# Scaling of streamed units moved from ScalarE to GpSimd, and the halo's edge copied from the halo buffer one tile later

## The chip, the cores and the metric

The kernel runs on one core of a Trainium2 chip. The metric is the device time of one execution in microseconds (us), which the slowest core sets; here there is one core. Lower is better.

## The reference

The input x is (1, 16, 2048, 2048) in float32. Two layers follow each other:

```
x = x + conv(groupnorm(x), weight)     # 8 groups of 2 channels; depthwise 6 x 11, causal: the
                                       # lower triangle of input and output alone is kept
x = x + groupnorm(x) + bias            # bias[c, i, j] = table[i - j], from a small MLP, per channel
```

The second line is `out = x * s + (bias + t)` with two numbers s and t for each group of channels. They are known only once the whole group has gone through the convolution. The part of x above the diagonal is not changed by the first line, but it too takes the second.

## The kernel before

A group is two channels. A channel is cut into four bands of 512 rows: the partition is a row block of four rows, so a band is 128 partitions x 4 rows x columns. A band's lower part is walked in **tiles** of 118 new columns: 5, 9, 13 and 18 tiles for the four bands, 90 tiles a group, 720 in all. For each tile ScalarE normalizes (`norm`, line 553), GpSimd masks it where it lies on the diagonal (`mask_tile`, line 951, 42 of 90 tiles), TensorE transposes it (line 1033), ScalarE casts the result to a high half in f16 (`split_hi`, line 568), VectorE makes the low half (`split_lo`, line 707), TensorE runs 36 matmuls (line 1047), and VectorE masks and adds the result into x (`evict`, lines 720 and 722). XT, the transposed tile, has three buffers, as have psT and psY.

The convolution needs two columns of XT from the band above. They are kept in `halo`, one entry for each tile position t. GpSimd copies them into XT in front (`halo_from`, line 966) and takes the last two out afterwards (`halo_to`, line 974). Where a band's width is no whole number of tiles, the next band needs two columns of a tile position that this band does not have. They are moved between partitions by four small DMAs (`copy_edge`, lines 572 to 579), from the XT buffer of the band's last tile. This occurs for one tile of each channel (tiles 26 and 71 of a group), 16 times in all. XT's buffer is written again three tiles on, so `split_hi` of that tile waits for `edge_copied`.

All five engines run one program that is unrolled over the 90 tiles of a group and loops over groups. Each pass does three things at once: statistics of group g+1 (part A, VectorE line 735, loads into `abuf`), the convolution of group g (part B), and the second layer of group g-1 (part C). Part C has kept blocks that stay in memory (`finish_kept`, line 874) and 36 **streamed units** of 512 KB for each group. A unit is loaded by SyncE into one of four buffers `ubuf` (line 469), finished there, and stored by ScalarE's queue (`store_stream`, line 619). 13 of the 36 are finished on VectorE in one instruction (`finish_stream`, line 882). The other 23 take two: ScalarE multiplies by s (`scale_stream`, line 612), then GpSimd adds the bias (`add_bias`, line 982). Over 8 groups that is 184 units.

A planner (`plan`) gives each unit the tile at which it is loaded, finished and stored: the load is issued two tiles ahead, the store stands two tiles behind, and the next load into a buffer waits for that buffer's store. Each engine executes its own list in order. Within tile n ScalarE has: `split_hi(n+2)`, `norm(n+4)`, the edge's copy, two squares for the statistics (line 590), the scaling of a unit, stores. GpSimd has: `mask_tile(n+4)`, `halo_to(n+1)`, `halo_from(n+2)`, `add_bias` of a unit. So an engine that waits for a unit's load holds up its share of the tiles behind it.

Of the kernel before, what the change touches and what calls it, by code (L numbers as in the profile page):

```python
# [25 lines left out]
def preact_conv_kernel(nc, x, wflip, w1, b1, w2, b2, w3, b3, out):  # L26
# [12 lines left out]
    XC = P // K  # L39
# [203 lines left out]
    with ctx:  # L243
# [277 lines left out]
        def _(act):  # L521
# [38 lines left out]
            def split_hi(g, n):  # L560
                N = NT * g + n
                act.wait_ge(transposed, N + 1)
                wait(act, convolved, N - NB3 + 1)
                wait(act, halo_out, N - NB3 + 1)
                for e, _ in EDGES:
                    if n == e + NB3:
                        act.wait_ge(edge_copied, 16 * K * (NEDGE * g + edges_before(n)))
                nc.scalar.copy(XT[:, n % NB3, 0, :, 2:P + 2], psT[n % NB3][:, :, :]).then_inc(hi_ready, 1)  # L568

            def copy_edge(g, n, w):  # L570

                c, b, t = TILES[n]
                act.wait_ge(lo_ready, NT * g + n + 1)
                act.wait_ge(halo_zeroed, chan(g, c) + 1)
                piece_i, col = divmod(STEP, XC)
                for k in range(K):
                    act.dma_start(halo[XC * k:XC * k + w, t + 1, :, 0, :],
                                  XT[XC * k + col:XC * k + col + w, n % NB3, :, piece_i, P:P + 2]
                                  ).then_inc(edge_copied, 16)
# [27 lines left out]

            def scale_stream(g, u):

                v = ubuf[:, u % NUB, :, :]  # L610
                act.wait_ge(u_loaded[u % NUB], 16 * (g * (NU // NUB) + u // NUB + 1))
                nc.scalar.activation(v, v, ACT.Identity, scale=col(outp, 0)  # L612
                                     ).then_inc(u_scaled, 1)
# [8 lines left out]
            def stage(s, do_a, do_b, do_c, do_next):  # L622
                p, ga, gb, gc = plan(do_a, do_b, do_c, on_dve), s, s - 1, s - 2
                for n in range(NT):
# [16 lines left out]
                    if do_b:  # L641
                        for e, w in EDGES:
                            if e == n:
# [10 lines left out]
                    if do_c:  # L654
# [9 lines left out]
                        for u in range(NU):  # L664
                            if p.u[u] == n and not on_dve[u]:
                                scale_stream(gc, u)
# [263 lines left out]
        def _(pool):  # L930
# [37 lines left out]
            def halo_to(g, n):  # L968
# [4 lines left out]
                wait_alone(pool, lo_ready, N + 1)  # L973
                nc.gpsimd.tensor_copy(halo[:, t, :, :, :], XT[:, n % NB3, :, :, P:P + 2]).then_inc(halo_out, 1)  # L974

            def add_bias(g, u):
                c = STREAM[u][0]
                if u_before[0][u] == u_before[0][c * (NU // CPG)]:
                    wait_alone(pool, bias_shifted, chan(g, c) + 1)
                pool.wait_ge(u_scaled, N_POOL * g + u_before[0][u] + 1)  # L980
# [149 lines left out]
```

## Time and profile before

| | us |
|---|---|
| median of 3 runs | 2881.85 (2877.08 to 2887.26) |
| the profiled execution, its own time | 2876.63 |
| its span, first to last instruction | 2874.8 |
| TensorE / VectorE / ScalarE / GpSimd busy | 2028.4 / 2305.3 / 1675.5 / 1159.4 |
| granted TensorE clock, mean share of 2.4 GHz | 0.893 |
| moved by DMA | 916.67 MB, mean 319 GB/s |

Part B runs from about 144 to 2710 us. The passes of the loop repeat with a period of about 337 us. The last 165 us are part C of the last group alone. Rows name a group of instructions by line, engine and operation, with what it writes and reads (`out<-in`). "Idle before" is time in which the engine had nothing running just before them, with what ended it. ACT is ScalarE, DVE is VectorE, POOL is GpSimd, PE is TensorE and SP is SyncE; a name with q is the engine's sequencer, which also issues DMAs.

### The profile page before, as it was taken

How to read it: one execution, taken by the hardware profiler on the slowest of the kernel's cores; microseconds unless marked ns; L12 is line 12 of the kernel's file. 1: busy time of each engine (PE TensorE's matmuls, PEld its weight loads, DVE VectorE, ACT ScalarE, POOL GpSimd, SP SyncE). 2: the span in 40 equal slices, each digit the busy share in tenths (PEclk: the TensorE clock that was granted, in tenths of full speed). 3: DMA queues.
4: the chain of work that ended last, by engine and by line, in shares of the span. 5: the costliest groups of instructions: out<-in, count | busy, mean ns of one | idle time of the engine just before them, and what ended most of it. 6: DMA issues, size and time to landing. Idle time of an engine off the chain costs nothing.

```text
span 2874.8 us, 82154 instructions
## 1 busy us (share of the span) xinstructions
PE 2028.4 (71%) x28880; PEld 1920.2 (67%) x28880; DVE 2305.3 (80%) x4167; ACT 1675.5 (58%) x3051; POOL 1159.4 (40%) x1988
## 2 busy tenths in 40 slices
PE   4089887778677775878668776787768777888600
PEld 0089886777577775867668776677758677778500
DVE  6878888798787987889787997879888897858625
ACT  2067665666557564766556665566647656677621
POOL 1033224534435343353435433453533535555443
PEclk9999998999889998999889999899989999999855
DMA  8875848999799987999889997999979996788799
GB/s 255 305 250 191 297 159 315 382 345 341 261 395 350 366 318 274 394 343 361 293 302 383 339 351 279 360 375 346 343 278 410 327 382 239 277 292 308 274 350 346
DMA packets 319859, 916.67 MB, mean 319 GB/s; under 512 B 42864, under 2 KB 42864, under 8 KB 317520
## 3 DMA queue, kind: packets, MB, share of 16 engines
q1 hardware_dynamic: 203744, 595.03, 58.3%
q10 hardware_dynamic: 115840, 318.80, 28.9%
q14 instruction: 204, 1.67, 0.2%
q8 instruction: 71, 1.16, 0.2%
HBM read 594.18 MB, written 319.68 MB: 318 GB/s over the span
## 4 chain that ended last, share of the span: by engine, by line
DMA 32%; DVE 25%; issue 17%; PE 10%; ACT 9%; POOL 3%; ACTq 2%; SPq 1%; DVEq 0%; POOLq 0%
DMA ubuf<-in_x 8%; DVE entries L735 8%; PE psY L1047 8%; DMA out<-ubuf 7%; DVE kept_c_band L874 5%; DMA abuf<-in_x 4%; DMA out<-kept_c_band 4%; DMA kept_c_band<-in_x 4%; DVE XT L707 4%; DVE psY L720 3%; DMA halo<-XT 3%; ACT junk L590 2%; ACT XT L568 2%; PE psT L1033 2%; ACT xn L553 2%
## 5 line engine op out<-in xcount | busy, mean ns | idle before, releaser
L1047 PEld LDWEIGHTS psY<-wsplit,XT 128*128 128x128 f16 x25920 | 1635.3, 103 | 299.3 <-issue 98.7
L1047 PE MATMUL psY<-wsplit,XT 128*128 128x168 f16 (+5 forms) x25920 | 1661.4, 225 | 234.3 <-DVE band L722 98.3
L707 DVE TENSOR_TENSOR XT<-psT,XT 128x512 f16<-128x512 f32 x720 | 491.0, 682 | 357.0 <-ACT XT L568 355.4
L1033 PE MATMUL psT<-ident,xn 128*128 128x128 f32 x2880 | 496.3, 298 | 326.9 <-POOL xn L951 224.2
L568 ACT CAST XT<-psT 128x512 f16<-128x512 f32 x720 | 414.9, 576 | 530.7 <-PE psT L1033 252.8
L982 POOL TENSOR_TENSOR ubuf<-ubuf,bias 128x1024 f32<-128x1024 f32 x184 | 412.2, 2241 | 523.7 <-ACT ubuf L612 523.4
L735 DVE BATCH_NORM_STATS2 entries<-abuf 128x6 f32<-128x512 f32 x928 | 586.8, 680 | 43.0 <-DMA abuf<-in_x 42.5
L951 POOL TENSOR_TENSOR xn<-xn,mask 128x512 f32<-128x512 f32 x336 | 416.3, 1239 | 503.9 <-ACT xn L553 422.3
L1033 PEld LDWEIGHTS psT<-ident,xn 128*128 128x128 f32 x2880 | 328.1, 150 | 342.3 <-POOL xn L951 221.9
L974 POOL COPY halo<-XT 128x16 f16<-128x16 f16 x720 | 222.5, 309 | 643.3 <-DVE XT L707 630.9
L553 ACT ACTIVATE xn<-kept_c_band,normp 128x512 f32<-128x512 f32 (+2 forms) x496 | 398.6, 804 | 94.8 <-DMA kept_c_band<-in_x 78.3
L874 DVE SCALAR_TENSOR_TENSOR kept_c_band<-kept_c_band,outp,bias 128x1024 f32<-128x1024 f32 x224 | 345.5, 1555 | 38.6 <-ACT bias L662 38.6
L612 ACT ACTIVATE ubuf<-ubuf,outp 128x1024 f32<-128x1024 f32 x184 | 209.7, 1140 | 253.2 <-DMA ubuf<-in_x 169.5
L590 ACT ACTIVATE junk<-kept_c_band,cur 128x512 f32<-128x512 f32 (+2 forms) x464 | 311.9, 672 | 66.0 <-DVE kept_c_band L722 31.1
L722 DVE SCALAR_TENSOR_TENSOR kept_c_band<-psY,wback,kept_c_band 128x472 f32<-128x472 f32 (+3 forms) x496 | 343.8, 693 | 6.2
L882 DVE SCALAR_TENSOR_TENSOR ubuf<-ubuf,outp,bias 128x1024 f32<-128x1024 f32 x104 | 159.3, 1532 | 98.2 <-DMA ubuf<-in_x 65.8
L720 DVE TENSOR_TENSOR psY<-psY,mask 128x472 f32<-128x472 f32 (+2 forms) x336 | 203.7, 606 | 0.0
L553 ACT ACTIVATE xn<-band,normp 128x512 f32<-128x512 f32 (+1 forms) x224 | 174.3, 779 | 28.4 <-DVE normp L801 28.4
L966 POOL COPY XT<-halo 128x16 f16<-128x16 f16 x720 | 166.2, 231 | 31.1 <-PE psY L1047 27.3
L590 ACT ACTIVATE junk<-band,cur 128x512 f32<-128x512 f32 x192 | 132.0, 687 | 40.4 <-DVE cur L806 21.8
L722 DVE SCALAR_TENSOR_TENSOR band<-psY,wback,band 128x472 f32<-128x472 f32 (+2 forms) x224 | 150.4, 671 | 5.6
L590 ACT ACTIVATION_READ_ACCUMULATOR junk<-kept_c_band,cur 128x1 f32 x464 | 87.0, 188 | 0.0
(76 smaller groups left out, 440.7 us busy)
## 6 DMA issues: line engine op xcount, KB each, us to landing
abuf<-in_x SPq DMA_DIRECT2D x464, 512.0 KB, 7.0
out<-ubuf ACTq DMA_DIRECT2D x288, 512.0 KB, 6.1
kept_c_band<-in_x SPq DMA_DIRECT2D x224, 512.0 KB, 8.7
out<-kept_c_band ACTq DMA_DIRECT2D x224, 512.0 KB, 7.2
ubuf<-in_x SPq DMA_DIRECT2D x192, 512.0 KB, 6.3
band<-in_x SPq DMA_DIRECT2D x48, 1024.0 KB, 9.5
out<-band ACTq DMA_DIRECT2D x48, 1024.0 KB, 9.3
ubuf<-out SPq DMA_DIRECT2D x96, 512.0 KB, 7.0
```

What stands on the lines that cost most here:

```text
L553: last = nc.scalar.activation(to[:, :, 0:whole, :], slot(c, b)[:, :, x0:x0 + XC * whole].rearrange("p k (i c) -> p k i c", c=XC), ACT.Iden ...
L568: nc.scalar.copy(XT[:, n % NB3, 0, :, 2:P + 2], psT[n % NB3][:, :, :]).then_inc(hi_ready, 1)
L590: nc.scalar.activation(junk[:, 0:nr * (c1 - c0)].rearrange("p (r c) -> p r c", r=nr), slot(c, b)[:, r:r + nr, BW * q + c0:BW * q + c1], AC ...
L707: nc.vector.tensor_tensor(XT[:, n % NB3, 1, :, 2:P + 2], psT[n % NB3][:, :, :], XT[:, n % NB3, 0, :, 2:P + 2], ALU.subtract).then_inc(lo_r ...
L720: nc.vector.tensor_tensor(y, y, mask_at(b, t, c0, c1), ALU.mult).then_inc(conv_masked, 1)
L722: nc.vector.scalar_tensor_tensor(out=xs, in0=y, scalar=col(wback, c), in1=xs, op0=ALU.mult, op1=ALU.add, accum_out=sums[:, n:n + 1]).then_ ...
L735: last = nc.vector.bn_stats(entries[:, e, :], row(q, r))
L874: nc.vector.scalar_tensor_tensor(out=v, in0=v, scalar=col(outp, 0), in1=bias_at(blk, nr // 2 * h, nr // 2), op0=ALU.mult, op1=ALU.add).the ...
L951: nc.gpsimd.tensor_tensor(v, v, m, ALU.mult).then_inc(xn_ready, 1)
L982: nc.gpsimd.tensor_tensor(v, v, bias_at(STREAM[u]), ALU.add).then_inc(u_added, 1)
L1033: last = nc.tensor.transpose(psT[m][:, i, :], xn[:, m, i, :, :].rearrange("p k c -> p (k c)"), ident[:, :])
L1047: last = nc.tensor.matmul(psY[m][:, 0:rows, o + lo_c:o + hi_c], XT[:, m, xp, i, 2 - sh:2 - sh + P], wsplit[:, c, wp, K * sh:K * sh + rows, ...
```

## The change

Two parts. First, `scale_stream` goes from ScalarE's list; `add_bias` on GpSimd now waits for the unit's load, multiplies by s in place, waits for that instruction, and adds the bias. Second, `copy_edge` reads the two columns from the `halo` entry that `halo_to` has written, not from XT, and stands one tile later in ScalarE's list. It waits for `halo_out` in place of `lo_ready` and `halo_zeroed`. `split_hi` no longer waits for `edge_copied`. The `halo` entry that the DMA reads is overwritten by the next band, so `halo_to` waits for `edge_copied` there, twice a group.

```diff
@@ split_hi (ScalarE)
                 wait(act, halo_out, N - NB3 + 1)
-                for e, _ in EDGES:
-                    if n == e + NB3:
-                        act.wait_ge(edge_copied, 16 * K * (NEDGE * g + edges_before(n)))
                 nc.scalar.copy(XT[:, n % NB3, 0, :, 2:P + 2], psT[n % NB3][:, :, :]).then_inc(hi_ready, 1)
@@ copy_edge (ScalarE)
-                act.wait_ge(lo_ready, NT * g + n + 1)
-                act.wait_ge(halo_zeroed, chan(g, c) + 1)
+                act.wait_ge(halo_out, NT * g + n + 1)
                 piece_i, col = divmod(STEP, XC)
                 for k in range(K):
                     act.dma_start(halo[XC * k:XC * k + w, t + 1, :, 0, :],
-                                  XT[XC * k + col:XC * k + col + w, n % NB3, :, piece_i, P:P + 2]
-                                  ).then_inc(edge_copied, 16)
+                                  halo[XC * k + col:XC * k + col + w, t, :, piece_i, :]).then_inc(edge_copied, 16)
@@ stage (ScalarE)
                         for e, w in EDGES:
-                            if e == n:
+                            if e + 1 == n:
                                 copy_edge(gb, e, w)
...
-                        for u in range(NU):
-                            if p.u[u] == n and not on_dve[u]:
-                                scale_stream(gc, u)
@@ halo_to (GpSimd)
+                for e, _ in EDGES:
+                    if n > e and (c, t) == (TILES[e][0], TILES[e][2]):
+                        wait_alone(pool, edge_copied, 16 * K * (NEDGE * g + edges_before(n)))
                 nc.gpsimd.tensor_copy(halo[:, t, :, :, :], XT[:, n % NB3, :, :, P:P + 2]).then_inc(halo_out, 1)
@@ add_bias (GpSimd)
+                wait_alone(pool, u_loaded[u % NUB], 16 * (g * (NU // NUB) + u // NUB + 1))
+                flat_v = ubuf[:, u % NUB, :, :]
+                nc.gpsimd.tensor_scalar(flat_v, flat_v, col(outp, 0), None, ALU.mult).then_inc(u_scaled, 1)
                 pool.wait_ge(u_scaled, N_POOL * g + u_before[0][u] + 1)
                 v = unit_of(ubuf, u % NUB, STREAM[u])
                 nc.gpsimd.tensor_tensor(v, v, bias_at(STREAM[u]), ALU.add).then_inc(u_added, 1)
```

ScalarE's list in the loop, at the first edge of a group (tile 26), before. The third row is the issue of the edge's first DMA, and line 568 is the cast into XT:

```order
L568 CAST XT<-psT 128x4x128 [waits halo_out,convolved,transposed]
L553 ACTIVATE xn<-kept_c_band,normp 128x4x4x32 [waits transposed]
L577 DMA halo<-XT 2x2x2 [waits halo_zeroed,lo_ready]
L577 DMA halo<-XT 2x2x2 x3
L562 REGISTER_ALU
L567 REGISTER_ALU [waits halo_out,convolved,transposed]
L568 CAST XT<-psT 128x4x128 [waits edge_copied]
L553 ACTIVATE xn<-kept_c_band,normp 128x4x4x32 [waits transposed]
```

And of the changed kernel, where the cast is line 565 and the edge's DMA line 573:

```order
L565 CAST XT<-psT 128x4x128 [waits halo_out,convolved,transposed]
L553 ACTIVATE xn<-kept_c_band,normp 128x4x4x32 [waits transposed]
L565 CAST XT<-psT 128x4x128 [waits halo_out,convolved,transposed]
L553 ACTIVATE xn<-kept_c_band,normp 128x4x4x32 [waits transposed]
L573 DMA halo<-halo 2x2x2 [waits halo_out]
L573 DMA halo<-halo 2x2x2 x3
```

The cast that stood behind the four DMAs and waited for their landing now stands in front of them, and no cast waits for `edge_copied`.

GpSimd's list in the loop at a unit on diagonal tiles, before (974 and 966 are the two halo copies, 951 the mask, 982 the bias addition):

```order
L974 COPY halo<-XT 128x16 [waits halo_in,lo_ready]
L966 COPY XT<-halo 128x8x2 [waits convolved]
L980 REGISTER_ALU
L982 TENSOR_TENSOR ubuf<-ubuf,bias 128x1024 [waits u_scaled]
L947 REGISTER_ALU
L951 TENSOR_TENSOR xn<-xn,mask 128x512 [waits diag_normed]
```

And of the changed kernel (962 and 951 are the halo copies, 936 the mask, 970 the new scaling, 973 the addition):

```order
L962 COPY halo<-XT 128x16 [waits halo_in,lo_ready]
L951 COPY XT<-halo 128x8x2 [waits convolved]
L379 ISA
L970 TENSOR_SCALAR ubuf<-ubuf,outp 128x1024 [waits u_loaded0]
L971 REGISTER_ALU
L973 TENSOR_TENSOR ubuf<-ubuf,bias 128x1024 [waits u_scaled]
L932 REGISTER_ALU
L936 TENSOR_TENSOR xn<-xn,mask 128x512 [waits diag_normed]
```

GpSimd now waits for the load itself, and the mask and halo copies of the next tile stand behind two instructions of the unit where they stood behind one.

## Rows read from the trace of the kernel before

**Rows 1.** The page's busy times and shares of the span.

```profile
PE 2028.4 (71%) x28880; PEld 1920.2 (67%) x28880; DVE 2305.3 (80%) x4167; ACT 1675.5 (58%) x3051; POOL 1159.4 (40%) x1988
```

**Rows 2.** The page's chain that ended last, shares of the span.

```profile
DMA 32%; DVE 25%; issue 17%; PE 10%; ACT 9%; POOL 3%; ACTq 2%; SPq 1%; DVEq 0%; POOLq 0%
DMA ubuf<-in_x 8%; DVE entries L735 8%; PE psY L1047 8%; DMA out<-ubuf 7%; DVE kept_c_band L874 5%; DMA abuf<-in_x 4%; DMA out<-kept_c_band 4%; DMA kept_c_band<-in_x 4%; DVE XT L707 4%; DVE psY L720 3%; DMA halo<-XT 3%; ACT junk L590 2%; AC
```

**Rows 3.** Stage windows: width, PE PEld DVE ACT POOL busy, clock, DMA share, GB/s.

```profile
1140.00:1260.00 120.00, 98.70 (x1416) 95.33 (x1415) 96.73 (x179) 81.14 (x150) 55.46 (x97) 0.90 1.00 381
...
1340.00:1412.00 72.00, 51.63 (x730) 49.33 (x731) 62.77 (x115) 45.59 (x83) 35.77 (x56) 0.91 0.88 321
...
2710.00:2875.00 165.00, 0.59 (x2) 0.50 (x2) 74.16 (x63) 36.20 (x37) 54.78 (x23) 0.51 0.93 342
```

**Rows 4.** The waits: waiter <- releaser: us in total, times, longest.

```profile
POOL ubuf L982 <- ACT ubuf L612: 523.4, 136, 16.5
...
DVE XT L707 <- ACT XT L568: 355.4, 247, 6.2
...
PE psT L1033 <- POOL xn L951: 224.2, 88, 10.6
...
ACT ubuf L612 <- DMA ubuf<-in_x: 169.5, 53, 7.9
...
ACT XT L568 <- DMA halo<-XT: 80.8, 16, 6.2
...
ACT ubuf L612 <- DMA ubuf<-out: 39.7, 12, 5.5
```

**Rows 5.** Timeline at the first edge of a group: start, us, what, [idle before].

```profile
1197.92 1.28 DVE L882 SCALAR_TENSOR_TENSOR ubuf<-ubuf,outp,bias 128x1024 f32<-128x1024 f32 x1
...
1198.60 2.12 PE L1047 MATMUL psY<-wsplit,XT 128*128 128x148 f16 x36
...
1200.84 0.58 ACT L568 CAST XT<-psT 128x512 f16<-128x512 f32 x1 [5.67 <-DMA halo<-XT]
...
1203.59 0.58 PE L1047 MATMUL psY<-wsplit,XT 128*128 128x148 f16 x7 [0.74 <-DVE kept_c_band L722]
```

**Rows 6.** Timeline at a unit whose load lands late.

```profile
1240.85 1.15 ACT L612 ACTIVATE ubuf<-ubuf,outp 128x1024 f32<-128x1024 f32 x1 [5.08 <-DMA ubuf<-in_x]
1241.06 0.34 ACTq L619 DMA_DIRECT2D out<-ubuf  x1
...
1242.08 2.35 POOL L982 TENSOR_TENSOR ubuf<-ubuf,bias 128x1024 f32<-128x1024 f32 x1 [4.83 <-ACT ubuf L612]
...
1244.39 1.13 POOL L951 TENSOR_TENSOR xn<-xn,mask 128x512 f32<-128x512 f32 x1
...
1245.57 1.12 PE L1033 MATMUL psT<-ident,xn 128*128 128x128 f32 x4 [5.27 <-POOL xn L951]
```

**Rows 7.** The page's groups: count, busy us, mean ns, idle before.

```profile
L982 POOL TENSOR_TENSOR ubuf<-ubuf,bias 128x1024 f32<-128x1024 f32 x184 | 412.2, 2241 | 523.7 <-ACT ubuf L612 523.4
...
L874 DVE SCALAR_TENSOR_TENSOR kept_c_band<-kept_c_band,outp,bias 128x1024 f32<-128x1024 f32 x224 | 345.5, 1555 | 38.6 <-ACT bias L662 38.6
L612 ACT ACTIVATE ubuf<-ubuf,outp 128x1024 f32<-128x1024 f32 x184 | 209.7, 1140 | 253.2 <-DMA ubuf<-in_x 169.5
...
L882 DVE SCALAR_TENSOR_TENSOR ubuf<-ubuf,outp,bias 128x1024 f32<-128x1024 f32 x104 | 159.3, 1532 | 98.2 <-DMA ubuf<-in_x 65.8
```

**Rows 8.** GpSimd's instructions with one input, by line: busy us, mean ns.

```profile
L939 POOL TENSOR_SCALAR_AFFINE_SELECT mask<-mask 128x728 bf16<-128x728 bf16 x1 | 0.8, 792 | 0.1
...
L941 POOL TENSOR_SCALAR_AFFINE_SELECT ident<-ident 128x128 f32<-128x128 f32 x1 | 0.3, 293 | 0.0
```

**Rows 9.** Timeline: GpSimd and VectorE instructions that meet.

```profile
1025.08 1.80 DVE L882 SCALAR_TENSOR_TENSOR ubuf<-ubuf,outp,bias 128x1024 f32<-128x1024 f32 x1
...
1025.74 1.20 POOL L974 COPY halo<-XT 128x16 f16<-128x16 f16 x1
...
1027.26 0.20 POOL L974 COPY halo<-XT 128x16 f16<-128x16 f16 x1 [0.19 <-POOL XT L966]
```

More of the change, by code:

```diff
@@ L606, in store_kept @@
                               ).then_inc(kept_stored[(blk, h)], 16)
[L608 to L613, printed above, removed]
             def store_stream(g, u):
```

## The prediction, made before the changed kernel had run

> **What bounds the kernel now.** I read the busy times first: no engine is full, VectorE is nearest with 80% of the span, ScalarE has 58% and GpSimd 40% [rows 1]. The chain of work that ended last says the same: DMA has 32% of it, VectorE 25%, ScalarE 9% and GpSimd 3% [rows 2]. Of the DMA part, the loads and stores of the streamed units have 8% and 7%, and the edge's small DMAs 3%. So the kernel is bound by turns. The stage windows tell where [rows 3]: from 1140 to 1260 us the 16 DMA engines are busy throughout (share 1.00, 381 GB/s), from 1340 to 1412 they have 12% to spare, and in the last 165 us, which hold part C alone, 7%. What is won in the first of these windows is mostly given back to the transfers; in the others it may stay.
>
> Then I read the waits [rows 4]. Two of ScalarE's belong to this change. It waits 16 times for the edge's DMAs, 80.8 us in all, and before the scalings for their loads, 169.5 us in 53 waits and 39.7 us in 12 more. VectorE waits 355.4 us for ScalarE's cast, which is one of the things queued behind both. TensorE waits 224.2 us in 88 waits for GpSimd's mask, and that is the part that a longer GpSimd list can make worse.
>
> **The edge.** The four DMAs are still issued, and cost ScalarE's queue the same; only the wait goes. The place shows what the wait does [rows 5]: a convolution ends at 1200.72 (1198.60 + 2.12), the cast could not start before 1200.84 after 5.67 us of idle time, and the next convolution starts at 1203.59, so TensorE lost 2.9 us. Sixteen times 2.9 us are 46 us. The limits are 0, if every wait is taken up by a later one, and the 76 us that 3% of the chain nearly comes to (I take 0.026 x 2875) [rows 2]; the full 80.8 us is the same thing read from the waits. Half of the 16 lie in the window with full DMA engines, and I give these a quarter of 23 us and the other eight a little over half of it: **-20 us**. The new waits cost nothing: `halo_out` of that tile was already awaited by the cast of three tiles on, which now stands in front, and `edge_copied` on GpSimd is awaited many tiles after the DMAs. If that cover went, each would cost one landing of some 5 us, on 16 tiles.
>
> **ScalarE loses the scaling.** It loses 184 instructions of 1.140 us, 209.7 us, and the idle time before them, 253.2 us [rows 7]. The loads that it waited for are not gone, they are now awaited by GpSimd, which waited for them before too, behind ScalarE. The example shows all of it [rows 6]. The load lands at 1240.85, the scaling takes 1.15, the addition runs from 1242.08 for 2.35 us, the mask follows at 1244.39, and only then can TensorE transpose, at 1245.57 after 5.27 us. Here TensorE is held by the load and GpSimd, not by ScalarE; putting 1.14 us on GpSimd in place of ScalarE changes nothing in it. But note the store of another unit, issued at 1241.06, 0.2 us after the load had landed: it stood behind ScalarE's wait. A late load of one buffer thus delays the store that frees another, whose load is late in turn. That coupling goes, because ScalarE next waits for this unit two tiles later, at its store. In the chain, loads and stores of units are 15% of 2875, some 430 us, and ScalarE 9% [rows 2]. With 65 such waits of 3.2 us (209.2 / 65), I take a sixth of their sum for the coupling in the loop, -35 us, and -5 us for the last stretch with its 7% to spare: **-40 us** together. The limits are 0 and all 209 us.
>
> **GpSimd gains an instruction for each unit.** The trace has no such instruction on GpSimd. Two with one input give a line: 293 ns for 128 elements and 792 ns for 728 [rows 8], so 0.83 ns an element, 1.04 us for 1024. They are of another operation and partly of another type, so this is an estimate. From below 0.85 us (the slope alone), from above 2.24 us, the addition over the same elements with two inputs [rows 7]. I take 1.1 us, near the one-input rows, and 0.2 us for the wait between it and the addition, as before a copy that waits for another one on this engine (0.19) [rows 9]. Three kinds of units:
> - 65 late loads: the unit is done 1.3 us after landing plus the addition, before 1.14 + 0.08. Half of that reaches TensorE: 65 x 0.08 x 0.5, **+3 us**.
> - 48 units (184 - 136 waits [rows 4]) where GpSimd was the late one: each is 1.3 us later, and with it the next tile's mask and halo. A quarter reaches TensorE, since most tiles wait for something else: 48 x 1.3 x 0.25, **+16 us**.
> - 71 units where ScalarE was late for another reason than the load: GpSimd did nothing and can now go ahead. It is early, which nobody waits for: 0, at most 1.3 us each the other way.
>
> **The two engines meet.** VectorE's instructions with two inputs from memory take 1.28 us alone [rows 5], but 1.80 us where they meet a GpSimd instruction, and a GpSimd copy of 0.20 us takes 1.20 behind one [rows 9]. Over 224 and 104 of them the means are 1.555 and 1.532 us, so 62 + 26 = 88 us are lost on VectorE beside GpSimd's 1159.4 us of work [rows 1, 7], 0.076 for each of them. 184 x 1.1 = 202 us more give 15 us, and with half of it on the path **+8 us**; the limits are 0 and, with 2.24 us in place of 1.1 and all of it on the path, 31.
>
> The Trainium skill, SBUF — State Buffer, section "SBUF: two separate sides", states that VectorE and GpSimd share one pair of ports by an exclusive lock, held for a whole instruction, between a VectorE operation with two SBUF inputs and any GpSimd operation that reads SBUF. By that rule the trace agrees (1.80 for 1.28, 1.20 for 0.20), and it says that the one-input scaling locks as the addition does; the sum above already counts it fully. The Trainium skill, GPSIMD Engine Reference, section "Engine selection", calls GpSimd's one-input operations roughly line-rate; at its clock of 1.2 GHz that would be an estimate of 0.85 us, and the sum would come out 13 us lower. No row here shows it.
>
> **The sum.** -20 - 40 + 3 + 16 + 8 = -33 us. Against the profiled execution's own 2876.6 us that is 2843.6. It lies 5 us under the median of the runs, 2881.85, so against the median it is 2849, and I give **2850 us**.
>
> **Rivals.** (A) *GpSimd's list becomes the wait.* The three costs together are 65 x 0.5 x (m - 1.02) + 48 x 0.25 x (m + 0.2) + 184 x 0.038 x m, or 51.5 m - 30.8 us with the new instruction's duration m. At 1.1 that is 26, at 2.24 it is 85 against the 60 won: 2882 + 25 = **2907 us**. It decides from m = 1.76 us, which either the instruction itself or its meetings with VectorE can reach. For it: 224 us of TensorE's waits already end at GpSimd's mask. Against it: GpSimd is at 40%, and the one-input rows lie at half of that price. Chance 0.22. (B) *The transfers take it all.* In the window with DMA share 1.00 neither gain nor cost shows; if the rest of the loop behaves alike, or if gains and costs cancel, the time is **2882 us** within 8. For it: 32% of the chain is DMA and 916.67 MB have to be moved either way. Chance 0.14. (C) *ScalarE was the coupling of everything.* Edge 76 us, coupling 60 us in place of 40, costs 26: 2882 - 110 = **2772 us**, or 2790 where part of the edge's is given back. For it: VectorE's 355.4 us behind the cast. Against it: the load-late example, where TensorE waits for GpSimd in both kernels. Chance 0.12. (D) *The wait moves to the store and back.* If GpSimd finishes a late unit more than two tiles after its landing, ScalarE stands at `u_added` with its casts behind it. Tiles take 337 / 90 = 3.75 us, two are 7.5, and load to sum takes 3.6, so this needs a GpSimd already 4 us behind; it is part of A's price.
>
> **Chances and range.** My case has 0.52, with 2828 to 2870 for its own range. A measurement of this kernel tells 0.3%, some 9 us, from no change. Faster by more than that: my case but for a small part, and C: 0.63. Within it: nearly all of B and the fringes of A and of mine: 0.14. Slower: A but for its fringe, and a bit of B: 0.23. The range goes from 2800 us, which takes in half the way to C and the bound 0.85 us, to 2900 us, which takes in B, and A up to m = 2.1 (51.5 x 2.1 - 30.8 - 60 = 17).
>
> **What would show it.** Right: no wait of the cast for the edge's DMA; the new instruction at 1.0 to 1.3 us; ScalarE's busy time down by 210 to about 1466 us; GpSimd's up by some 200 to 1360; GpSimd's wait before the scaling for loads, about 170 to 210 us in 50 to 65 waits; the means of VectorE's lines 874 and 882 up from 1.55 to 1.60 to 1.65; stores no longer issued right at a landing; TensorE's wait for the mask between 200 and 260 us. Wrong: a duration over 1.76 us, TensorE's wait for the mask over 300 us, or ScalarE idle at a unit's store for more than 50 us in all. If the cast waits less and the time stays, B was right and the loads' waits on GpSimd and VectorE will have grown.

## The result and the profile after

The changed kernel takes 2954.88 us (median of 4 runs, 2949.85 to 2961.34), the kernel before 2884.56 (4 runs). The ratio is 1.0248, 95% interval [1.0216, 1.028]: 2.5% slower, 71 us at the 2877 us to which I refer all ratios below. Forecast were 2850 us and a range up to 2900. The profiled execution has a span of 2959.6 us.

The page's busy times and its chain, engines first and then the first lines:

```profile
PE 2048.0 (69%) x28880; PEld 1950.5 (66%) x28880; DVE 2356.0 (80%) x4167; ACT 1490.3 (50%) x2867; POOL 1687.0 (57%) x2172
...
DVE 27%; DMA 21%; issue 17%; POOL 15%; PE 13%; ACT 5%; SPq 1%; ACTq 1%; POOLq 0%; DVEq 0%
...
PE psY L1038 10%; POOL ubuf L970 9%; DVE entries L720 9%; DVE kept_c_band L859 5%; DMA ubuf<-in_x 5%; DMA abuf<-in_x 4%; DMA out<-kept_c_band 4%; DVE XT L692 4%; PE psT L1024 3%; DVE psY L705 3%; DMA out<-ubuf 3%; DMA out<-band 3%; POOL ubuf L973 2%; POOL xn L936 2%; ACT junk L585 1%
```

Against [rows 1] ScalarE is busy 185 us less. That is short of the 210 us that its scalings take by their own durations, since in the trace of before they overlap their neighbours by 21 us. GpSimd is busy 528 us more, where some 200 were expected. Against [rows 2] DMA falls from 32 to 21% of the chain and GpSimd rises from 3 to 15%, of which the new scaling alone has 9.

GpSimd's groups, shapes kept apart (busy us, mean ns, then the idle time before them and what ended it):

```profile
L970 POOL TENSOR_SCALAR ubuf<-ubuf,outp 128x1024 f32<-128x1024 f32 x184 | 552.0, 3000 | 198.9 <-ACT bias L650 91.4 <-DMA ubuf<-in_x 89.3 <-DMA ubuf<-out 18.0
L973 POOL TENSOR_TENSOR ubuf<-ubuf,bias 128x1024 f32<-128x1024 f32 x184 | 421.6, 2292 | 15.4
L936 POOL TENSOR_TENSOR xn<-xn,mask 128x512 f32<-128x512 f32 x336 | 414.1, 1232 | 462.9 <-ACT xn L553 386.9 <-ACT xn L556 75.0
```

The new instruction takes **3.00 us, not 1.1**. It is longer than the addition with two inputs over the same unit (2.29 here, 2.24 before), which I had taken as its upper bound. The rest of GpSimd's difference is small.

The waits (waiter, releaser, us in total, times, longest) show who pays:

```profile
ACT XT L565 <- PE psT L1024: 552.0, 324, 6.1
...
DVE XT L692 <- ACT XT L565: 367.8, 249, 6.5
...
PE psT L1024 <- POOL xn L936: 321.2, 85, 10.8
...
ACT XT L565 <- POOL halo L962: 107.4, 55, 7.5
...
POOL ubuf L970 <- DMA ubuf<-in_x: 89.3, 25, 7.4
...
PE psY L1038 <- POOL XT L951: 72.3, 43, 4.7
```

The cast's wait for the edge's DMA (80.8 us in [rows 4]) is gone, as meant. But TensorE's wait for the mask has grown from 224.2 to 321.2 us, and the freed ScalarE spends its time waiting for TensorE's transposes. GpSimd itself waits less for loads than forecast (89.3 us in 25 waits, plus 18.0 for loads from the output), because it comes to most of them late.

Two windows, with the columns of [rows 3]:

```profile
1160.00:1280.00 120.00, 97.21 (x1411) 93.53 (x1408) 97.21 (x177) 69.08 (x137) 84.81 (x109) 0.91 0.96 365
2782.00:2960.00 178.00, 0.83 (x8) 0.64 (x5) 81.77 (x64) 10.37 (x15) 130.86 (x46) 0.51 0.87 317
```

The first lies at the same place of the program as 1140:1260 before, some 20 us on. The transfers, which had filled it (share 1.00, 381 GB/s), now leave 4% idle, and GpSimd's busy time has gone from 55 to 85 us of 120. The second begins where the last convolution ends, at 2782.2 where it was 2709.2. So 73 us of the span's 85 are lost in the loop. Of the other 12, the last part is 178 us long in place of 166, with GpSimd busy for 131 us where it was 55: there it is the one that the last stores wait for.

What happens in the loop, from the timeline of the changed kernel (start, us, what, and in brackets the idle time before):

```profile
1245.22 2.84 POOL L970 TENSOR_SCALAR ubuf<-ubuf,outp 128x1024 f32<-128x1024 f32 x1
...
1247.57 1.28 DVE L867 SCALAR_TENSOR_TENSOR ubuf<-ubuf,outp,bias 128x1024 f32<-128x1024 f32 x1
...
1248.14 2.56 POOL L973 TENSOR_TENSOR ubuf<-ubuf,bias 128x1024 f32<-128x1024 f32 x1
...
1250.66 1.12 POOL L936 TENSOR_TENSOR xn<-xn,mask 128x512 f32<-128x512 f32 x1
...
1251.84 1.12 PE L1024 MATMUL psT<-ident,xn 128*128 128x128 f32 x4 [4.20 <-POOL xn L936]
...
1252.99 0.59 ACT L565 CAST XT<-psT 128x512 f16<-128x512 f32 x1 [4.43 <-PE psT L1024]
...
1253.61 0.69 DVE L692 TENSOR_TENSOR XT<-psT,XT 128x512 f16<-128x512 f32 x1 [3.57 <-ACT XT L565]
```

The scaling did not wait for its load: GpSimd came to it straight from a halo copy. Scaling and addition hold GpSimd for 5.5 us, more than a tile's 3.75. The mask stands behind both, TensorE is idle for 4.20 us, and ScalarE and VectorE in a row behind it. In the trace of before, GpSimd came to a unit with less than 0.1 us of idle time in 46 of 184 cases, in the changed kernel in 136.

The late addition holds up ScalarE by a second way. A unit's store stands in ScalarE's list two tiles on, and it waits for the addition:

```profile
705.41 0.63 PE L1024 MATMUL psT<-ident,xn 128*128 128x128 f32 x4
...
706.02 2.34 POOL L973 TENSOR_TENSOR ubuf<-ubuf,bias 128x1024 f32<-128x1024 f32 x1
...
708.52 0.91 ACTq L607 DMA_DIRECT2D out<-ubuf  x2
...
708.87 2.46 PE L1038 MATMUL psY<-wsplit,XT 128*128 128x148 f16 x21 [2.83 <-POOL XT L951]
...
709.61 0.59 ACT L565 CAST XT<-psT 128x512 f16<-128x512 f32 x1 [4.78 <-issue]
```

The cast's tile was transposed at 706.04, the addition ended at 708.36, then came the store, and only then the cast. Counted so over the timeline, ScalarE stood in front of 55 stores before the last convolution, for 112 us in all, each time with a cast as its next work. In 33 of them that cast's tile was already transposed, for 45 us. In the trace of before there is no such case ahead of the last convolution.

TensorE also got a lower clock. The mean granted share is 0.872 where it was 0.893, and its 28880 matmuls are busy 2048.0 us where they were 2028.4. The windows at the example above show the clock at its upper level (2.4 GHz), while TensorE stands idle from 706.04 to 708.87, and then at its lower one (share 0.50, 1.2 GHz):

```profile
706.00:708.00 2.00, 0.04 (x1) 0.00 (x0) 2.00 (x4) 0.00 (x0) 1.98 (x1) 0.98 0.16 64
708.00:710.00 2.00, 1.13 (x12) 1.13 (x13) 2.00 (x5) 0.39 (x1) 1.98 (x6) 0.50 0.67 197
```

How much of the 71 us this makes was not separated from the waits.

### The profile page after: what moved, and what is told of

Same layout as the page of the kernel before. It is cut to its first block, busy times and chain, and to the rows that moved or that the text cites. A ratio compares the mean times of both kernels' runs of the same rounds, so it can differ in the third digit from the quotient of the medians.

```text
span 2959.6 us, 82322 instructions
## 1 busy us (share of the span) xinstructions
PE 2048.0 (69%) x28880; PEld 1950.5 (66%) x28880; DVE 2356.0 (80%) x4167; ACT 1490.3 (50%) x2867; POOL 1687.0 (57%) x2172
## 4 chain that ended last, share of the span: by engine, by line
DVE 27%; DMA 21%; issue 17%; POOL 15%; PE 13%; ACT 5%; SPq 1%; ACTq 1%; POOLq 0%; DVEq 0%
PE psY L1038 10%; POOL ubuf L970 9%; DVE entries L720 9%; DVE kept_c_band L859 5%; DMA ubuf<-in_x 5%; DMA abuf<-in_x 4%; DMA out<-kept_c_band 4%; DVE XT L692 4%; PE psT L1024 3%; DVE psY L705 3%; DMA out<-ubuf 3%; DMA out<-band 3%; POOL ubuf L973 2%; POOL xn L936 2%; ACT junk L585 1%
## 5 line engine op out<-in xcount | busy, mean ns | idle before, releaser
L1038 PEld LDWEIGHTS psY<-wsplit,XT 128*128 128x128 f16 x25920 | 1664.9, 104 | 322.5 <-issue 117.9
L1038 PE MATMUL psY<-wsplit,XT 128*128 128x168 f16 (+5 forms) x25920 | 1686.8, 226 | 264.5 <-DVE kept_c_band L707 87.1
L1024 PE MATMUL psT<-ident,xn 128*128 128x128 f32 x2880 | 502.2, 301 | 350.5 <-POOL xn L936 321.2
L970 POOL TENSOR_SCALAR ubuf<-ubuf,outp 128x1024 f32<-128x1024 f32 x184 | 552.0, 3000 | 198.9 <-ACT bias L650 91.4
L962 POOL COPY halo<-XT 128x16 f16<-128x16 f16 x720 | 203.5, 283 | 528.5 <-DVE XT L692 510.6
L973 POOL TENSOR_TENSOR ubuf<-ubuf,bias 128x1024 f32<-128x1024 f32 x184 | 421.6, 2292 | 15.4
L859 DVE SCALAR_TENSOR_TENSOR kept_c_band<-kept_c_band,outp,bias 128x1024 f32<-128x1024 f32 x224 | 362.9, 1633 | 42.2 <-ACT bias L650 42.2
L867 DVE SCALAR_TENSOR_TENSOR ubuf<-ubuf,outp,bias 128x1024 f32<-128x1024 f32 x104 | 171.1, 1649 | 107.3 <-DMA ubuf<-in_x 68.0
L951 POOL COPY XT<-halo 128x16 f16<-128x16 f16 x720 | 154.6, 215 | 51.3 <-PE psY L1038 47.1
L650 ACT ACTIVATE bias<-bias,outp 128x3587 f32<-128x3587 f32 x16 | 52.4, 3278 | 121.7 <-DMA bias<-bias_scratch 84.8
```

The source lines that it names most:

```text
L859: nc.vector.scalar_tensor_tensor(out=v, in0=v, scalar=col(outp, 0), in1=bias_at(blk, nr // 2 * h, nr // 2), op0=ALU.mult, op1=ALU.add).the ...
L970: nc.gpsimd.tensor_scalar(flat_v, flat_v, col(outp, 0), None, ALU.mult).then_inc(u_scaled, 1)
L973: nc.gpsimd.tensor_tensor(v, v, bias_at(STREAM[u]), ALU.add).then_inc(u_added, 1)
L1024: last = nc.tensor.transpose(psT[m][:, i, :], xn[:, m, i, :, :].rearrange("p k c -> p (k c)"), ident[:, :])
L1038: last = nc.tensor.matmul(psY[m][:, 0:rows, o + lo_c:o + hi_c], XT[:, m, xp, i, 2 - sh:2 - sh + P], wsplit[:, c, wp, K * sh:K * sh + rows, ...
```

## The experiments

Theory A: the time follows the duration m of GpSimd's new instruction, as rival A's formula has it, and only m was wrong. Rivals: the edge part or its waits did harm; the scaling's place (its wait for the load in front of masks) did, whatever its duration; 3.00 us comes from VectorE's company or from the factor being read from memory. Ratios are each to runs of the kernel before on the same chip.

### The two parts apart

The edge alone: the changed kernel with the scaling back on ScalarE.

```diff
+                        for u in range(NU):
+                            if p.u[u] == n and not on_dve[u]:
+                                scale_stream(gc, u)
...
-                wait_alone(pool, u_loaded[u % NUB], 16 * (g * (NU // NUB) + u // NUB + 1))
-                flat_v = ubuf[:, u % NUB, :, :]
-                nc.gpsimd.tensor_scalar(flat_v, flat_v, col(outp, 0), None, ALU.mult).then_inc(u_scaled, 1)
```

> The edge's part alone, the scaling as before. Theory P (the price of the new GpSimd instruction makes the whole loss, 3.0 us where 1.1 was taken): the edge part keeps its own small gain, 2862 to 2880 us against 2884 of before, ratio 0.993 to 0.999, and the cast's wait for the edge's DMA (80.8 us) is gone. Rival E (the edge's copy at its new place, and the waits that it adds on GpSimd, cost something): over 2890 us. Rival B (the wait is taken up by later ones): ratio within 0.002 of 1.

Measured: 2865.58 us, ratio 0.9949 [0.9935, 0.9963], **-15 us**. The wait for the edge's DMA is gone, no wait for it shows on GpSimd, and ScalarE's wait for loads has grown from 169.5 us [rows 4], which is where a part of it went:

```profile
DVE XT L702 <- ACT XT L565: 318.5, 230, 6.2
...
PE psT L1031 <- POOL xn L946: 215.2, 80, 10.6
...
ACT ubuf L607 <- DMA ubuf<-in_x: 194.5, 49, 7.0
```

The scaling alone: the kernel before, with the three lines above on GpSimd and `scale_stream` gone from ScalarE.

> The scaling's part alone, the edge as before. Theory P: 2955 plus what the edge part gives, so 2960 to 2980 us, and the instruction at 3.0 us. Rival E: below 2945 us, since the edge part would have been part of the loss.

Measured: 2988.2 us, ratio 1.0389 [1.0373, 1.0405], **+112 us**, a little over the range of the first expectation. With the edge part beside it, it is 1.0248. So the scaling makes all of the loss, and the edge part never harms. It is even worth more beside the slow scaling, 41 us by the ratios (1.0389 less 1.0248), than alone. Why more was not tried.

### The duration of the new instruction, by doses

Without the multiplication: GpSimd waits for the load at the same place, then adds, so these units lack the factor s. VectorE's wait for a group's scalings becomes one for its additions.

```diff
-                nc.gpsimd.tensor_scalar(flat_v, flat_v, col(outp, 0), None, ALU.mult).then_inc(u_scaled, 1)
...
-                pool.wait_ge(u_scaled, N_POOL * g + u_before[0][u] + 1)
```

> The changed kernel with the multiplication of the 184 units left out altogether: GpSimd waits for the load and adds the bias, ScalarE does nothing for them, so these units' output lacks the factor s. It is m = 0 in the prediction's formula. Theory P: GpSimd's busy time decides, so the time falls below that of before, to 2800 to 2860 us. Rival W (GpSimd's wait for the load at its place in the list, not the instruction's length, makes the loss): still over 2900 us.

Measured: 2823.55 us, ratio 0.9804 [0.9788, 0.9819], **-56 us**. Place, wait and order are those of the changed kernel; what costs is the multiplication with its handover to the addition. That the place alone did it is refuted. GpSimd's wait for loads is now as long as ScalarE's had been, and TensorE's for the mask is back under [rows 4]:

```profile
PE psT L1021 <- POOL xn L936: 199.6, 81, 10.3
...
POOL ubuf L970 <- DMA ubuf<-in_x: 169.1, 42, 10.1
```

Durations by themselves: the kernel before, and at its end, with the other engines done, single GpSimd instructions on the units' buffers, twice each (here two of them).

```diff
+                step(nc.gpsimd.tensor_scalar(dst[:, 0:w], src[:, 0:w], col(outp, 0), None, ALU.mult))
+                step(nc.gpsimd.tensor_copy(dst[:, 0:w], src[:, 0:w]))
```

> The kernel before, with twenty GpSimd instructions added behind its end, each alone and waiting for the one before: scaling with a factor from memory over 256, 512 and 1024 float32 elements, scaling and adding with a constant, copy, and a product of two inputs over 512 and 1024. Only their durations are asked for. Theory P1 (the factor from memory makes it slow): 2.8 us with it over 1024 and about 1.1 with a constant. Theory P2 (any one-input arithmetic of this operation is slow on GpSimd): 2.8 with both, and the copy at 1.0. Theory P3 (the place, with other work around it, made it slow): about 1.1 for all here, since nothing runs beside it.

The groups of that stretch, shapes apart:

```profile
L1020 POOL TENSOR_SCALAR ubuf<-ubuf,outp 128x1024 f32<-128x1024 f32 x2 | 5.7, 2842 | 0.2
L1027 POOL TENSOR_SCALAR ubuf<-ubuf 128x1024 f32<-128x1024 f32 x2 | 5.5, 2774 | 0.2
L1022 POOL TENSOR_SCALAR ubuf<-ubuf 128x1024 f32<-128x1024 f32 x2 | 5.5, 2768 | 0.2
L1026 POOL TENSOR_TENSOR ubuf<-ubuf 128x1024 f32<-128x1024 f32 x2 | 4.7, 2339 | 0.2
L1020 POOL TENSOR_SCALAR ubuf<-ubuf,outp 128x512 f32<-128x512 f32 x2 | 3.1, 1562 | 0.2
...
L1024 POOL COPY ubuf<-ubuf 128x1024 f32<-128x1024 f32 x2 | 2.1, 1040 | 0.1
```

Line 1020 multiplies by the factor in memory, 1022 by a constant, 1027 adds a constant. All three take 2.77 to 2.84 us. So neither the factor's place nor the operation nor the company makes the 3.00 us, but the form: two lengths give (2842 - 1562) / 512 = 2.5 ns an element. Only the copy runs at the 1.04 us that my line through the AFFINE_SELECT rows [rows 8] gave. VectorE's company adds the difference from 2.84 to 3.00: 35 of the change's 184 scalings start while VectorE is in an addition, and last 3.67 us on the mean, the others 2.84.

The changed kernel with a copy in its place, at the duration that the prediction reckoned with:

```diff
-                nc.gpsimd.tensor_scalar(flat_v, flat_v, col(outp, 0), None, ALU.mult).then_inc(u_scaled, 1)
+                nc.gpsimd.tensor_copy(flat_v, flat_v).then_inc(u_scaled, 1)
```

> The changed kernel with GpSimd's scaling replaced by a copy of the same unit onto itself: the factor is left out of the computation, and the instruction takes about 1.04 us (as its mean alone on GpSimd) in place of 3.0. This is the kernel that the prediction reckoned with (m = 1.1). By the prediction's sum: 2850 less 3 for the shorter instruction, 2840 to 2855. By a straight line between the run without scaling (2823.6 at m = 0) and the change (2955 at m = 3.0): 2869. If GpSimd's slack takes the first microsecond for nothing (a kink rather than a line): 2825 to 2835.

Measured: 2848.91 us, ratio 0.991 [0.9875, 0.9944], **-26 us**. The prediction said -33 for m = 1.1, and the first of the three expectations came. The copy takes 1.14 us in company:

```profile
L970 POOL COPY ubuf<-ubuf 128x1024 f32<-128x1024 f32 x184 | 210.0, 1141 | 270.1 <-DMA ubuf<-in_x 118.3 <-ACT bias L650 87.6 <-DMA ubuf<-out 63.8
```

And with a product of two tensors, the factor broadcast:

```diff
+                nc.gpsimd.tensor_tensor(flat_v, flat_v, col(outp, 0).unsqueeze(2).to_broadcast([P, 2, BW]), ALU.mult).then_inc(u_scaled, 1)
```

> The changed kernel with the scaling written as a product of two tensors, the factor broadcast along the unit; alone on GpSimd a product of 1024 elements took 2.34 us against 2.84 for the scaling by a factor. If the time follows the duration of GpSimd's added instruction, at 44 us per us of it: 0.5 us less is 22 us less, 2928 to 2940. If it is not the duration but where the instruction stands (its wait for the load ahead of the masks), 2950 to 2958. If VectorE's company lengthens a two-input product more than a scaling, its mean is at 2.6 to 3.0 and the time is within 10 us of the change's.

Measured: 2919.28 us, ratio 1.0161 [1.012, 1.0202], **+46 us**, at m = 2.00:

```profile
L970 POOL TENSOR_TENSOR ubuf<-ubuf,outp 128x1024 f32<-128x1024 f32 x184 | 368.8, 2004 | 195.1 <-ACT bias L650 97.7 <-DMA ubuf<-in_x 63.9 <-DMA ubuf<-out 33.3
```

The product with a broadcast factor is a microsecond shorter than the scaling by a factor, and 25 us faster by the ratios, where the expectation's 44 us for each microsecond would give 44; it also reckoned with 2.34 us for the product, not 2.00. The time lies under its 2928. Each row of this table has its cost counted from the run without multiplication (ratio less 0.9804, times 2877), and beside it rival A's 51.5 m - 30.8 with the m of its trace:

| GpSimd's new instruction | m, us | ratio | cost measured, us | 51.5 m - 30.8 |
|---|---|---|---|---|
| none | 0 | 0.9804 | 0 | (not below 0) |
| copy | 1.14 | 0.991 | 30 | 28 |
| product, two inputs | 2.00 | 1.0161 | 103 | 72 |
| scaling, one input | 3.00 | 1.0248 | 128 | 124 |

The two instructions with one input lie near the formula. The product lies 31 us above it. VectorE may be why, which was not tested: it is busy 2410.3 us there, against 2329.5 without multiplication, 2351.6 with the copy and 2356.0 with the scaling. TensorE's clock changes with the dose too: its busy time is 2005.2 us without multiplication (granted share 0.897) and 2048.0 with the scaling (0.872). How much of these 43 us is in the cost of 128 no run tells. VectorE's finishing additions, line 859, with the copy and with the product:

```profile
L859 DVE SCALAR_TENSOR_TENSOR kept_c_band<-kept_c_band,outp,bias 128x1024 f32<-128x1024 f32 x224 | 370.4, 1667 | 38.6 <-ACT bias L650 38.6
```

```profile
L859 DVE SCALAR_TENSOR_TENSOR kept_c_band<-kept_c_band,outp,bias 128x1024 f32<-128x1024 f32 x224 | 395.9, 1780 | 38.7 <-ACT bias L650 38.7
```

### What the relief of ScalarE is made of

The prediction took its -40 us from a coupling: stores stand behind ScalarE's wait for a load. So, with the edge part and the scaling on ScalarE, the stores now come first within each tile (`store_kept` and `store_stream` ahead of `scale_stream`).

> The edge part alone, with the scaling back on ScalarE, but in each of ScalarE's tiles the stores are now issued ahead of the scaling with its wait for a load. It tells what of the gain of the run without scaling (2823.6, against 2865.6 of the edge alone: 42 us) came from stores that no longer stand behind load waits, and what from ScalarE's 210 us of work. Theory C (coupling, as the prediction took it: a store held up by a load's wait delays the next load into its buffer): most of the 42 us comes back, 2830 to 2850. Theory W (it is ScalarE's busy time, or the turns of the other engines): 2860 to 2872, as the edge part alone. Under C the stretches at full DMA share become longer; under W ScalarE's wait for loads only stands elsewhere in its list.

Measured: 2858.96 us (12 runs, 2840.84 to 2866.68), ratio 0.9945 [0.9925, 0.9965]. That is the edge alone, 0.9949. A gain over it of much more than 7 us (0.9949 less 0.9925, the interval's lower end) is unlikely. But the edit takes only a part of the coupling away: a store still stands behind the load's wait of the tile before. Ahead of the last convolution, the edge alone has a store issued right behind a scaling's wait for 160 us of 176, this run for 81 of 197. Half of the coupling was worth nothing that shows; that the whole was worth 40 us is unlikely, and not excluded by this run alone.

Then the wait kept in place and most of the work taken away:

```diff
-                nc.scalar.activation(v, v, ACT.Identity, scale=col(outp, 0)
+                nc.scalar.activation(v[:, :, 0:32], v[:, :, 0:32], ACT.Identity, scale=col(outp, 0)
```

> The edge part alone; ScalarE still waits for each load at the same place, but then scales only 64 of the unit's 1024 elements: the factor is left out for the other 960. So ScalarE keeps its waits for loads and loses some 165 us of its 210 us of scaling. It splits the 42 us between the edge alone (2865.6, ratio 0.9949) and the run without scaling (2823.6, ratio 0.9804). Theory W (ScalarE's work counts, not its wait): most of it comes back, ratio 0.981 to 0.986, 2823 to 2837 us. Theory C (the wait in ScalarE's list counts): ratio 0.991 to 0.995, 2850 to 2863. GpSimd's additions can start earlier here too, which by both theories is worth little, since it waited 554 us for the scaling and had slack.

Measured: 2839.93 us, ratio 0.9874 [0.9855, 0.9893], between the two theories. The group shows how much was really removed:

```profile
L607 ACT ACTIVATE ubuf<-ubuf,outp 128x64 f32<-128x64 f32 x184 | 62.5, 341 | 322.2 <-DMA ubuf<-in_x 214.0 <-DMA ubuf<-out 59.0 <-issue 27.5
```

The factor is left out for 960 of the 1024 elements. 147 of 210 us of work are gone, 70%, and 22 of the 42 us came back (by the two intervals 15 to 29), while ScalarE's idle time there grew to 322 us. So with the waits kept, about half of the relief comes back. It is put down to ScalarE's work, though GpSimd's addition also starts 0.8 us sooner here. What the rest owes to the wait in its list and what to the remaining 62.5 us of work, this run does not tell.

### Both engines burdened

The edge alone, and on GpSimd ahead of each addition three scalings of a scratch tile, which do not depend on the load:

```diff
+                for i in range(3):
+                    wait_alone(pool, pad_done, 3 * k + i + 1)
+                    nc.gpsimd.tensor_scalar(pad[:, :], pad[:, :], 1.5, None, ALU.mult).then_inc(pad_done, 1)
```

> The edge part alone with the scaling on ScalarE as before, and on GpSimd ahead of each bias addition three scalings of 256 elements of a scratch tile of their own, about 2.8 us and three handovers, 3.2 us per unit in all: GpSimd's list gets as long as in the change, without a wait for a load and without the dependence of the addition on its own scaling. If GpSimd's occupation is what costs, and ScalarE's relief was worth 42 us in the change too: 2955 + 42 = 2997, up to 3010 with the handovers, ratio 1.038 to 1.050. If the change lost by GpSimd's waits for loads in front of the next mask, which this kernel does not have: 2930 to 2965. If in the change ScalarE's relief is worth nothing since GpSimd sets the pace: 2950 to 2970.

Measured: 2931.47 us, ratio 1.0211 [1.0179, 1.0242], that is +75 us over the edge alone. It lies in the range of the second expectation (2930 to 2965), which put a part of the change's loss down to loads awaited in front of the mask, and under the other two. GpSimd spends as much on it as on the change's scaling: 529.6 us busy, 57.7 of handovers, and 41.2 of waiting for ScalarE ahead of the addition.

```profile
L985 POOL TENSOR_SCALAR pad<-pad 128x256 f32<-128x256 f32 x552 | 529.6, 959 | 158.2 <-ACT bias L659 100.3 <-POOL pad L985 57.7 <-issue 0.2
L988 POOL TENSOR_TENSOR ubuf<-ubuf,bias 128x1024 f32<-128x1024 f32 x184 | 422.9, 2299 | 41.6 <-ACT ubuf L609 41.2
```

One thing follows: GpSimd's occupation costs 75 us with no load in front of it, and TensorE's wait for the mask is 306.2 us here, 215.2 in the edge alone. The change is 11 us slower by the ratios, which is within the two intervals (13 us), so this kernel, with ScalarE's 210 us of scaling in it, is about as fast. Two readings fit. Either ScalarE's relief is worth nothing once GpSimd is late, or the change's burden is some 50 us heavier than this one and the relief of 42 us hides it. For the second: these three scalings can run while the load is under way, since GpSimd's wait for ScalarE ahead of the addition is down from 541.8 us in the edge alone to 41.2, and the change's scaling cannot start before the landing. VectorE is also busy 44 us less here (2312.3). No run separates the two.

### A version with the scaling divided

> A version that might beat both kernels: the edge part, and of each stage's 23 units that GpSimd adds the bias to, it scales only the 7 (units 6, 8, 9, 10, 21, 22 and 24) behind which the next tiles whose masks it applies are furthest off; ScalarE scales the other 16. If GpSimd has room at these places, ScalarE's relief is worth 56 of 184 units of the 42 us: 13 us under the edge alone, ratio 0.990. If the 3.0 us fall on the path there too, at the change's 44 us per us for 184 units: 56/184 of 131 us, less 13 us: 27 us over the edge alone, ratio 1.004.

The diff decides per unit from the table of diagonal tiles, with a semaphore of its own for GpSimd's scalings:

```diff
+    by_pool = [not on_dve[u] and not any(is_diag[(STEADY.u[u] + AHEAD + i) % NT] for i in (1, 2, 3)) for u in range(NU)]
```

Measured: 2873.18 us, ratio 0.9988 [0.9974, 1.0002]: 11 us worse than the edge alone, between the two expectations. So even there GpSimd's 56 scalings of 2.88 us cost more than ScalarE's relief gives. It is not the mask that pays: TensorE waits 207.0 us for it, 215.2 in the edge alone. But its wait for GpSimd's halo copy grows from 43.4 to 87.0 us, and it is busy 2034.8 us at a granted share of 0.880, where it was 2018.0 at 0.893. The fastest kernels with the full computation are the edge alone and the edge with the stores first, 0.5% under the kernel before, and equal.

## Why the prediction was wrong

The step that failed is one term: "I take 1.1 us, near the one-input rows", with 2.24 us as its upper bound. Measured were 3.00 us, above the bound. It put me under the 1.76 us from which rival A decides, and on the wrong side. The rest, by its steps:

- **The edge**, -20 us: measured -15 alone. Right, with its waits at no cost. The 2.9 us of its example hold 0.66 us of transposes, so TensorE stood idle for 2.2.
- **ScalarE's loss**, -40 us: the run without multiplication gains 42 us over the edge alone. The size was right, its mechanism is not confirmed: with half of the stores' waits behind loads gone nothing could be measured, and with 70% of ScalarE's work gone about half of the 42 us came back. Whether the change itself still had this gain is open.
- **GpSimd's burden and the meetings**, with m left open: 51.5 m - 30.8. At m = 1.14 the formula gives 28 and the copy costs 30; at 3.00 it gives 124 and the change costs 128. For the copy the sum would be -20 - 40 + 28 = -32 us, measured -26 [-36, -16]. For the change it would be 2882 + 124 - 60 = 2946 us, measured 2954.88. So the sum held at these two doses and its input did not. It did not hold at the others: at m = 2.00 the product costs 31 us more, and at m = 0 the sum would be -20 - 40 - 31 = -91 us, measured -56. Within the formula the shares were off in ways that may cancel: it counts 48 late units, where 136 are late in the change, and a fixed quarter of each reaching TensorE. It holds no term for ScalarE's stand at the stores, nor for the clock. That it fits at two doses is luck in part and no proof of its terms.
- **The meetings** were priced for 1.1 us at +15 us on VectorE. The two additions that it was taken from (lines 874 and 882 before, 859 and 867 after) are busy 534.0 us where they were 504.8: 29 us more with 528 us more GpSimd work, 0.055 for each, where 0.076 was taken. VectorE's other 22 us lie in small instructions that the term did not cover. The run without multiplication already has 17 of the 29 us with no more GpSimd work, so more than half of them come with GpSimd's changed order and not with the scaling.
- **Rival A** is what happened, at a price beyond its 2907 us, since that was worked out at the bound of m. Its two signs came: duration over 1.76 us, TensorE's wait for the mask over 300 us (321.2). **Rival D** came in too, and well over the 50 us that I had named as its sign: counted from the timeline, ScalarE stood in front of a unit's store until GpSimd's addition ended for 196 us in all, where it was 28 in the trace of before. Of these, 84 us in 21 stores lie behind the last convolution, where no cast stands behind the store, and 112 us in 55 stores ahead of it, where one does. With the copy those 112 are 21. I had called it a part of A's price, but the formula has no term for it. **Rival B** fell: the window with full transfers now has them at 0.96. **Rival C** is bounded by the run without multiplication: with the instruction free, no more than 56 us are to be had, not 110.

The bound was the mistake in method. I took the addition with two inputs as the dearest thing that an instruction with one input could be. Nothing in the profile said so; the two rows that made my line were of another operation. Both ends of the range for m were on instructions of other kinds, and the chance of 0.22 for rival A counted on that bound.

The Trainium skill, GPSIMD Engine Reference, section "Engine selection", has one-input operations on GpSimd roughly at line rate. This case's measurement agrees for the copy (1040 ns for 1024 elements) and differs for the scaling (2842 ns), which is what the change used. Here the measurement decides. The Trainium skill, SBUF — State Buffer, section "SBUF: two separate sides", says that of VectorE's operation with two inputs and GpSimd's, whichever starts first holds the ports for its whole instruction. The trace agrees where VectorE is first, all but 0.12 us:

```profile
438.41 1.27 DVE L859 SCALAR_TENSOR_TENSOR kept_c_band<-kept_c_band,outp,bias 128x1024 f32<-128x1024 f32 x1
438.49 3.91 POOL L970 TENSOR_SCALAR ubuf<-ubuf,outp 128x1024 f32<-128x1024 f32 x1
```

The scaling ends 2.72 us after the addition. Where the one-input scaling is first, it agrees for the first 0.9 us of the scaling and not for its whole length. An addition that starts early is held up, one that starts later is not:

```profile
1006.54 2.84 POOL L970 TENSOR_SCALAR ubuf<-ubuf,outp 128x1024 f32<-128x1024 f32 x1 [7.37 <-DMA ubuf<-in_x]
...
1006.75 1.98 DVE L859 SCALAR_TENSOR_TENSOR kept_c_band<-kept_c_band,outp,bias 128x1024 f32<-128x1024 f32 x1
```

```profile
485.08 2.84 POOL L970 TENSOR_SCALAR ubuf<-ubuf,outp 128x1024 f32<-128x1024 f32 x1
...
486.64 1.28 DVE L859 SCALAR_TENSOR_TENSOR kept_c_band<-kept_c_band,outp,bias 128x1024 f32<-128x1024 f32 x1
```

The second pair runs side by side at the lengths that both have alone. In scalings of 2.84 us, the 44 additions of VectorE that start 0.89 us or more behind the scaling's start take 1.27 to 1.30 us, and the 12 that start within 0.79 us take 1.40 to 2.15 and end 0.65 us ahead of the scaling.

## What to carry to other kernels

Before an instruction is moved to GpSimd, its form must be found in a trace or timed by itself: there a scaling by one factor costs more than a product of two tensors, and a copy less than half of either. When the one price that a sum needs is missing, work out from which price the sign turns, and give that side weight according to how little the rows say, not according to where the nearest row happens to lie. And an engine at 40% of the span may have no room: what counts is what stands behind the added instruction in its list, here a mask that TensorE waits for, and what other engines' lists wait for it, here ScalarE's stores with casts behind them.

## What the runs showed of the hardware

- GpSimd's scalar arithmetic on f32 is slow whatever its scalar is: 2842 ns with the factor in memory, 2768 with a constant, 2774 for an addition, at 1024 elements, about 2.5 ns an element; the two-tensor product 2339, the copy 1040.
- A product with a broadcast operand took 2004 ns in company, against 2339 alone for two full operands.
- GpSimd's work of one input adds little to VectorE's time, its work of two inputs clearly more: VectorE is busy 2329.5 us without multiplication, 2351.6 with the copy, 2356.0 with the scaling and 2410.3 with the product.
- A GpSimd scaling of 1024 elements (2.84 us) holds up VectorE's two-input addition only if that one starts in its first 0.8 us: 1.40 to 2.15 us in 12 cases, 1.27 to 1.30 in the 44 that start from 0.89 us on.
